# Layer 1's scans: u times D as matmuls, y copied out by ScalarE, four transfer slots, spread diagonals and piecewise loads

## The reference, cut to what matters

```
dA = exp(dt[:, :, None] * A)
h  = dA * h + (dt * u)[:, :, None] * B[:, None, :]
y  = einsum('bdn,bn->bd', h, C) + D * u
yh = y1 + y2 + y3 + y4        # y3, y4 turned back
```

## Time and profile before

| | us |
|---|---|
| median of 3 runs | 18361.85 (18345.74 to 18377.84) |
| the profiled execution's own time | 18362.69 |
| its span, first to last instruction | 18360.9 |
| busy over the span: PE, DVE, ACT, POOL | 16077.0, 15910.4, 14529.2, 11254.5 |
| mean granted TensorE clock | 0.962 |

### The profile page before, as it was taken

The page is one execution under the profiler, slowest core; times in us unless marked ns, Lnnn a source line. Parts: engine busy times, 40 slices in busy tenths (PEclk is TensorE's granted clock), DMA queues, the critical chain, the costliest instruction groups (busy, mean ns, idle before and its releaser), DMA issues. The chain is left out here.

```text
span 18360.9 us, 268147 instructions
## 1 busy us (share of the span) xinstructions
PE 16077.0 (88%) x94216; PEld 11444.0 (62%) x94216; DVE 15910.4 (87%) x12063; ACT 14529.2 (79%) x23238; POOL 11254.5 (61%) x6343
## 2 busy tenths in 40 slices
PE   8799998899996788879888888888888888889798
PEld 3355554455552365455688888888888888647374
DVE  4799998799996486479899999999999999879698
ACT  7699996799992555557899999999999999745556
POOL 0099993499990475035688888888888888500201
PEclk9899999899997899989999999999999999999899
DMA  5788886788879677767777777777777777741323
GB/s 178 231 243 250 246 252 208 233 249 247 251 223 245 213 226 217 265 230 278 224 191 200 194 192 191 194 193 192 191 190 197 197 191 191 194 122 55 104 57 101
DMA packets 1043305, 3693.66 MB, mean 201 GB/s; under 512 B 162006, under 2 KB 196410, under 8 KB 1017404
## 3 DMA queue, kind: packets, MB, share of 16 engines
q1 hardware_dynamic: 815420, 3003.46, 53.8%
q0 software_dynamic: 147456, 536.94, 14.9%
q10 hardware_dynamic: 79104, 136.10, 2.4%
HBM read 2342.15 MB, written 796.94 MB: 171 GB/s over the span
## 5 line engine op out<-in xcount | busy, mean ns | idle before, releaser
L1832 DVE TENSOR_TENSOR_SCAN l1s_h<-l1s_da,l1s_pd 128x1024 f32<-128x1024 f32 x3072 | 6709.3, 2262 | 152.0 <-DMA l1s_h<-l1s_h 85.4
L1853 ACT ACTIVATE l1s_da<-l1s_dl,l1s_a 128x1024 f32<-128x1024 f32 x3072 | 3505.0, 1141 | 312.7 <-DVE l1s_h L1832 308.5
L1718 PE MATMUL l1s_pd<-l1s_bd,l1s_dut 128*128 128x128 f32 x18432 | 2847.5, 291 | 853.7 <-DVE l1s_h L1832 828.6
L1718 PEld LDWEIGHTS l1s_pd<-l1s_bd,l1s_dut 128*128 128x128 f32 x18432 | 2297.3, 191 | 1229.0 <-DVE l1s_h L1832 1092.0
L1870 ACT ACTIVATE l1s_dm<-l1s_dut,l1s_bt 128x384 f32<-128x384 f32 x5120 | 2888.2, 602 | 200.9 <-PE l1s_pd L1723 200.5
L1687 POOL TENSOR_TENSOR l1s_pb<-l1s_h,l1s_cc 128x1024 f32<-128x1024 f32 x1024 | 2423.4, 2367 | 843.7 <-DVE l1s_h L1832 802.6
L1687 POOL TENSOR_TENSOR l1s_pa<-l1s_h,l1s_cc 128x1024 f32<-128x1024 f32 x1024 | 2428.0, 2371 | 84.1 <-DMA l1s_h<-l1s_h 84.1
L1723 PE MATMUL l1s_pd<-l1s_id,l1s_dm 128*128 128x128 f32 x15360 | 2186.6, 273 | 0.1
L2702 POOL TENSOR_TENSOR l0sf_pr<-l0sf_h,l0sf_cc 128x1024 f32<-128x1024 f32 x768 | 1810.9, 2375 | 32.2 <-DVE l0sf_h L2784 27.0
L2702 POOL TENSOR_TENSOR l0sb_pr<-l0sb_h,l0sb_cc 128x1024 f32<-128x1024 f32 x768 | 1809.1, 2371 | 30.8 <-DVE l0sb_h L2784 26.8
L1723 PEld LDWEIGHTS l1s_pd<-l1s_id,l1s_dm 128*128 128x128 f32 x15360 | 1789.4, 142 | 0.6 <-ACT l1s_dm L1870 0.5
(11 more groups left out here) (323 smaller groups left out, 31362.7 us busy)
## 6 DMA issues: line engine op xcount, KB each, us to landing
l1s_cc<-crows SPq DMA_DIRECT2D x1024, 512.0 KB, 4.5
l1s_h<-l1s_h POOLq DMA_DIRECT2D x1024, 512.0 KB, 6.9
l0sf_cc<-l0crowsf SPq DMA_DIRECT2D x512, 512.0 KB, 6.3
l0sb_cc<-l0crowsb SPq DMA_DIRECT2D x512, 512.0 KB, 5.7
l0sf_cc<-l0crowsf SPq DMA_DIRECT2D x512, 256.0 KB, 8.5
l0sb_cc<-l0crowsb SPq DMA_DIRECT2D x512, 256.0 KB, 7.6
dls<-l1p_dl SPq DMA_DIRECT2D x192, 512.0 KB, 7.0
duts<-l1p_dut SPq DMA_DIRECT2D x64, 1536.0 KB, 6.6
```

Source lines behind the costliest of these rows:

```text
L1718: pe.matmul(pd[:, s % 2, blk * 128:blk * 128 + 128], dut[:, half, blk, j * 128:j * 128 + 128], bd[:, n, blk - SCALED, :], start=True, stop ...
L1832: dve.tensor_tensor_scan(tile(rnd, j), da[:, j, :], pd[:, s % 2, :], 0.0, ALU.mult, ALU.add)\
L1853: act.activation(da[:, j, :], dl[:, half, j, :], ACT.Exp, scale=a[:, HT * half + j, n:n + 1])\
```

## The change

All edits but the last are in `l1_scans`.

- The term u x D moves to TensorE: matrices `dg` with the summed D on the diagonal are made once, and in rounds 24 to 27, step 0, `add_skip` adds the products of `u` with them to `py`, four blocks a round.
- `finish` moves from VectorE to ScalarE and becomes a plain copy of `py` to `yo`, at steps (2,1) and (3,2). TensorE's first accumulations of an image move to (2,2), (3,0), (4,0) and (4,1).
- The ring of the tile of step 1 grows from two to four, and `s_sum` from two to four semaphores.
- The diagonals of states 0 to 7 are made in rounds 17, 19, ... 31 of the image before, those of 8 to 15 in rounds 1, 3, ... 13 and 14. They wait for `bt` alone, which has semaphores of its own and is loaded in SyncE's round 5 (second half) and round 16 (first half of the next image). TensorE now waits itself for the loads of a half.
- The other loads are split: `dut` in four, `dl` in three, `u` in two pieces, one piece a round, from round 5 (nine pieces) and from round 18 (seven).
- ScalarE's products for the next round are split 1, 2, 2 over the steps in both halves.
- All 32 images are written out, with no loop.

```diff
-    STEP_BLOCKS = ((range(0, 1), range(1, 3), range(3, 5)), (range(0, 2), range(2, 4), range(4, 5)))
+    HALF_BLOCKS = (range(0, BLOCKS // 2), range(BLOCKS // 2, BLOCKS))
+    STEP_BLOCKS = (range(0, 1), range(1, 3), range(3, 5))
-    RINGS = (4, 2, 2)
-    TOGETHER = 3
-    LOADS = (3 * 16, 4 * 16)
+    RINGS = (4, 4, 2)
+    SUMS = 4
+    PIECES = (7, 9)
...
+        def diagonal_round(n):
+            return min(2 * n - (N - 1), N - 2)
...
         def images(eng, body):
-            body(0, True, False)
-            for i in range((IMAGES - 2) // TOGETHER):
-                for k in range(TOGETHER):
-                    body(i * TOGETHER + (k + 1), False, False)
-            body(IMAGES - 1, False, True)
+            for b in range(IMAGES):
+                body(b, b == 0, b == IMAGES - 1)
...
+                def load(b, half, piece):
+                    if piece < 4:
+                        at = piece * (BLOCKS // 4)
+                        cols = slice(at * HT * 128, (at + BLOCKS // 4) * HT * 128)
+                        sp.dma_start(dut[:, half, at:at + BLOCKS // 4, :],
+                                     duts[bass.ds(b, 1), half, :, cols].rearrange("a p n -> p (a n)")).then_inc(s_in[half], 16)
+                    elif piece < 7:
+                        sp.dma_start(dl[:, half, piece - 4, :], one(dls[:, HT * half + piece - 4], b)).then_inc(s_in[half], 16)
+                    else:
+                        sp.dma_start(u[:, piece - 7, :], one(u1[:, piece - 7], b)).then_inc(s_in[half], 16)
+
+                def load_bt(b, half):
+                    sp.dma_start(bt[:, half, :, :], bts[bass.ds(b, 1)].rearrange("a p n -> p (a n)")).then_inc(s_bt[half], 16)
...
                         if rnd == 5 and not first:
-                            load(b, 1)
-                        if rnd == 20 and not final:
-                            load(b + 1, 0)
+                            load_bt(b, 1)
+                        if 5 <= rnd < 5 + PIECES[1] and not first:
+                            load(b, 1, rnd - 5)
+                        if rnd == 16 and not final:
+                            load_bt(b + 1, 0)
+                        if 18 <= rnd < 18 + PIECES[0] and not final:
+                            load(b + 1, 0, rnd - 18)
...
+                def add_skip(b, part):
+                    j, blocks = part // 2, HALF_BLOCKS[part % 2]
+                    if part == 0:
+                        pe.wait_ge(skipd, nth(5))
+                        loaded(pe, b, 1)
+                    for blk in blocks:
+                        mm = pe.matmul(py[:, j, blk * 128:blk * 128 + 128], u[:, j, blk * 128:blk * 128 + 128], dg[:, j, :],
+                                       start=False, stop=False, skip_group_check=True)
...
-                        if j == 1 and not (first and rnd < 2):
-                            dve.wait_ge(s_sum[rnd % 2], summed(*((b, rnd - 2) if rnd > 1 else (b - 1, rnd + ROUNDS - 2))))
+                        if j == 1 and not (first and rnd < SUMS):
+                            dve.wait_ge(s_sum[rnd % SUMS], summed(*((b, rnd - SUMS) if rnd >= SUMS else (b - 1, rnd + ROUNDS - SUMS))))
...
-                        if rnd == 2 and j == 0 and not first:
-                            finish_b(b - 1)
-                        if rnd == 3 and j == 0 and not first:
-                            finish_a(b - 1)
...
+                def diagonals(b, n):
+                    if not (isinstance(b, int) and b == 0):
+                        act.wait_ge(trd, nth((b - 1) * STEPS + (N + n) * HT + HT - 1))
+                    act.wait_ge(s_bt[0], b * 16 + 16)
+                    for blk in range(SCALED, BLOCKS):
+                        ins = act.activation(bd[:, n, blk - SCALED, :], idt[:, :], ACT.Identity, scale=bt[:, 0, blk, n:n + 1])
+                    ins.then_inc(diagd, 1)
...
+                def finish(b, j, rows, back, fin):
+                    act.wait_ge(back, nth(b))
+                    act.activation(yo[rows, j * HW:j * HW + HW], py[rows, j, :], ACT.Identity).then_inc(fin, 1)
...
                             decay(b, rnd * HT + j)
                             if not first and (rnd, j) == (1, 1):
                                 hold(b - 1, 1, yb, heldb)
+                            if not first and (rnd, j) == (2, 1):
+                                finish_b(b - 1)
                             if not first and (rnd, j) == (2, 2):
                                 hold(b - 1, 0, ya, helda)
+                            if not first and (rnd, j) == (3, 2):
+                                finish_a(b - 1)
                             if ahead:
                                 times_b(m, v, blocks)
+                            if j == 0:
+                                for n in range(N):
+                                    if diagonal_round(n) % ROUNDS == rnd and not (final and diagonal_round(n) < 0):
+                                        diagonals(b if diagonal_round(n) >= 0 else b + 1, n)
```

More of the change, by code:

```diff
@@ L1601, in l1_scans @@
         s_in = [r.dma_sem(f"in{s}") for s in range(2)]
+        s_bt = [r.dma_sem(f"bt{s}") for s in range(2)]
         s_cc = [r.dma_sem(f"cc{s}") for s in range(4)]
@@ L1668, in _ @@
                 for half in range(2):
-                    load(0, half)
+                    load_bt(0, half)
+                    for piece in range(PIECES[half]):
+                        load(0, half, piece)
                 for rnd in range(3):
@@ L1715, in turn @@
                     pe.wait_ge(scan, nth(b * STEPS + s - 2))
-                    pe.wait_ge(diagd, nth(b * N + (N - 1 if half else n)))
+                    if n == 0 and j == 0:
+                        loaded(pe, b, half)
+                    pe.wait_ge(diagd, nth(b * N + n))
                     for blk in range(SCALED, BLOCKS):
@@ L1808, in _ @@
                 dve.wait_ge(skipd, nth(2))
-                def finish(b, j, rows, back, fin):
-                    dve.wait_ge(back, nth(b))
-                    dve.scalar_tensor_tensor(out=yo[rows, j * HW:j * HW + HW], in0=u[rows, j, :], scalar=dsum[rows, j, 0:1],
-                                             in1=py[rows, j, :], op0=ALU.mult, op1=ALU.add).then_inc(fin, 1)
-                def finish_b(b):
-                    finish(b, 1, slice(0, DHIGH), backb, finb)
-                def finish_a(b):
-                    finish(b, 0, slice(0, DLOW), backa, fina)
+                dve.memset(dg[DHIGH:, 1, :], 0.0).then_inc(skipd, 1)
+                for j, rows in ((0, slice(0, DLOW)), (1, slice(0, DHIGH))):
+                    dve.tensor_scalar(dg[rows, j, :], idt[rows, :], dsum[rows, j, 0:1], None, ALU.mult).then_inc(skipd, 1)
                 def body(b, first, final):
@@ L1860, in times_b @@
                             loaded(act, b, half)
-                        if half == 0:
-                            if not (isinstance(b, int) and b == 0):
-                                act.wait_ge(trd, nth((b - 1) * STEPS + (N + n) * HT + HT - 1))
-                            for blk in range(SCALED, BLOCKS):
-                                ins = act.activation(bd[:, n, blk - SCALED, :], idt[:, :], ACT.Identity,
-                                                     scale=bt[:, half, blk, n:n + 1])
-                            ins.then_inc(diagd, 1)
+                            act.wait_ge(s_bt[half], b * 16 + 16)
                         act.wait_ge(trd, nth(b * STEPS + (rnd - 1) * HT - 1))
@@ L1885, in body @@
                         m, v = b + (rnd + 1) // ROUNDS, (rnd + 1) % ROUNDS
-                        for j, blocks in enumerate(STEP_BLOCKS[v // N]):
+                        for j, blocks in enumerate(STEP_BLOCKS):
                             decay(b, rnd * HT + j)
@@ L3096 @@
     out = nc.dram_tensor("out", (IMAGES, C, HW), F32, kind="ExternalOutput").ap()
-    with nc.semaphore("sums0") as even, nc.semaphore("sums1") as odd:
-        build(nc, aps.pop("x"), aps, out, [even, odd])
+    with ExitStack() as stack:
+        build(nc, aps.pop("x"), aps, out, [stack.enter_context(nc.semaphore(f"sums{k}")) for k in range(4)])
     r = run_bass_kernel_spmd(nc, [{f"in_{name}": a for name, a in arrays.items()}], core_ids=[0])
```

47 lines of the change are left out of this document (24 added, 23 removed).

## The result

The changed kernel takes 18868.72 us (median of 4 runs, 18846.15 to 18884.48), the one before 18356.37 (4 runs). The ratio is 1.0279, 95% interval 1.0266 to 1.0291: slower, by 512 us. I had predicted 18,785, in the range 18,600 to 18,940.

What follows compares the result with a forecast made beforehand. VectorE's scans were taken to bound the stage; 18362.7 - 249.6 (gains) + 616.9 (A, B and C over 31 images) + 55.8 (clock) = 18785.8, given as 18,785 us, range 18,600 to 18,940.

Steps and rivals of the forecast that it cites:

- B: ScalarE's round 15 waits for the last piece of u; scan 46 late by 4.6 us an image, ends 2.5 to 6.7.
- C: ScalarE's round 17 diagonals wait for the next image's bt; scan 52 late by 11.1 us, ends 9.6 to 12.9.
- Rival 1: Pieces of the loads are in time, only gains show: 18,113 us, or 18,243 with A charged; chance 0.05.
- Rival 2: One of the two load waits is hidden: 18,615 us with C alone, 18,414 with B alone; chance 0.13.
- Rival 3: TensorE's clock stays low for a round after every hole and TensorE bounds there: +254, 19,040 us; chance 0.12.
- the decay as releaser: Sign on VectorE: its idle before scans should be released by the decay (l1s_da), some 600 us.
- Finishes off VectorE: Each image's two finishing instructions leave VectorE: 81.6 busy plus 54.2 waiting, 135.8 us saved.
- The 28.4 us of "issue": VectorE idle in 24 stretches before scans, put to the low clock after holes; all 28.4 us saved.
- Ring of four: Scans' wait on VectorE for the transfer folding two h tiles goes, with smaller pieces helping: all 85.4 us saved.
- A: ScalarE's copies out wait for TensorE's transposes back, making scans late: 4.2 us an image, ends 2.1 to 6.
- The clock: TensorE's granted clock drops after the holes of B and C: 0.9 us for each of 62, 55.8 in all.
- u x D on TensorE and the written-out images: Added TensorE products at step 0 of four rounds, and images as straight-line code: both taken as 0.

Runs made afterwards that it cites:

- x3: Changed kernel with both edits, next image's diagonals from round 21 and second half's loads from round 2, so no load is late: 18227.75 us.
- x1: Changed kernel with the diagonals of the next image's states 0 to 5 made from round 21 on, not 17, so bt is in time: 18528.53 us.
- x2: Changed kernel with the second half's bt and nine pieces issued from SyncE's round 2, not 5: 18579.61 us.
- x6: Kernel before with only the ring of four for step 1's tile and four semaphores for the transfer: 18385.46 us against 18357.27.
- x9: Kernel before with only the loads in pieces, from rounds 2 and 18, ring of two kept: 18246.80 us, ratio 0.9926.
- x10: x6 with the big loads whole but issued in different rounds (5, 7, 9 and 20, 22): 18231.89 us, ratio 0.9918 to the kernel before.
- x4: x3 with the first copy out moved on ScalarE behind round 2's third decay and the held copy, step (2,2): 18118.00 us.
- x7: x4 with the ring of step 1's tile and the transfer's semaphores back at two: 18148.18 us.
- x8: x3 with u x D and the finish back on VectorE, no products of u on TensorE: 18200.67 us.
- x5: Changed kernel with the last piece of u issued ahead of the spread of C in SyncE's round 13: 18758.96 us.

## Why the prediction was right, and where its terms were off

The mechanism was right: ScalarE comes to two loads before SyncE, which is behind it, has issued them (in the image shown 1.4 and 7.5 us before, 12053.39 and 12077.24), and both waits are shown by removing them one at a time. That the sum came within 84 us was in part luck: B and C both lay outside the ends that I had given for them, on opposite sides. Rival 1 (the pieces are in time) fell: x3 shows what it would have looked like, 18,228, near the 18,243 given for it. Rival 2 (one hidden) fell: each wait is there 31 times, and x1 and x2 add up in x3. Rival 3 fell too: the clock was back within the next round.

Of the signs, the decay as releaser (608.9 us), the 31 waits for bt (11.3 us each, 13 said) and the clock (0.95) came out; the 31 waits for u were 11.1 us each, where 6 to 8 had been said. Point by point, against the terms of the sum, with the totals of the stage from the section on the result:

- Finishes off VectorE, -135.8: they are gone from the list after, but were worth less in the stage. In the image of the earlier trace rows the first scan behind each starts 2.4 and 1.5 us later than the usual step of 2.18, which is 123 us for the 31 pairs that stand among the scans; the last pair stands behind them.
- The 28.4 us of "issue", said to be the clock's: 15.7 of them were five stretches of the kind that x6 shows, a scan behind GpSimd's wait for its spread. So the 1.2 us a hole that was read from them priced two things at once.
- Ring of four, "85.4 us, all of it": the amount is gone from the profile after, but the step gave it to the ring, and that was wrong. Alone the ring loses 28 us (x6), the loads apart make the gain (x9, x10), and the ring adds some 30 (x4 against x7). I had looked at who waits for the transfer and not at what else stood in SyncE's queue behind the same loads.
- A, 4.2 an image: 2.06 + 0.67 + 0.95 + 0.70 + 0.23 = 4.6 in the image shown, and 4.6 in all others: 13 us more. That the move gives nothing back was right (x8). Of it 3.5 us was the place of one copy (x4).
- B, 4.6 an image, 6.7 at most: measured 8.0 in the mean, and this is the term that was mis-sized most: 247.3 - 142.6 = 105 us. In the image shown it was 8.76: the piece landed 10.5 us after its issue, 10.9 after the spread's, not 6.6. I had taken 4.2 us a MB from a 1.5 MB load of before; this half MB took 4.7 us more than the spread, and the spread itself 6.2. x5 says that issuing it ahead of the spread takes 3.5 us off. How the rest divides between spread, piece and GpSimd's transfer (11.0 us here, 6.9 in the median before) was not measured by itself and stays open.
- C, 11.1 an image: measured 8.55 in the mean, since bt landed some 4 us after its issue and not 5.6. My lower end, that it lands with the spread, gave 9.6; in the image shown both landed together, but the spread took 3.6 us and not 4.5. That is 344.1 - 265.1 = 79 us less. The Trainium skill's fit ("DMA: Bandwidth & Descriptors", section "Anatomy of one DMA") gave 2.2 us for bt and so 7.6 for C, 1 us too low; the page gives it for a transfer that GpSimd issues, and bt is issued by SyncE. The trace has 3.5 us for bt here and 4.0 in the median of the stage.
- The clock, 0.9 a hole: 0.69 + 0.63 and 0.69 + 0.89 in the image shown, but 1.84 in the mean of all 62, twice what was said: 114.3 - 55.8 = 58 us more. The 0.66 had been taken from the first of the late scans, behind a hole of 2.39 us; here the second is late too, mostly by more than the first.
- u x D on TensorE and the written-out images, 0: in x4 the whole stage has 25 us of idling behind its first scan, so neither can cost more than that.

Together 105 - 79 + 13 + 58 = 97 us over the forecast. The stage grew by 531 where the sum had 423, 108 over; the finishes (13 us less gained) are about the rest. That the whole time is only 84 over (18,869 against 18,785) comes in part from the shorter work ahead of the stage, which no term of mine foresaw. B and C, off in opposite directions, hid most of each other.

## What to carry to other kernels

When each engine works down a list of its own, "round 16" is a different time on each. Before a load is moved, write down for its issuer and for its first reader when each reaches that round, from rows of the profile, and take the landing time between; here the issuer ran 4.9 us behind a round's end and the reader 3 to 4 us ahead of its start, and two waits of some 8 us an image on VectorE made a change that would have gained 132 us (x3) lose 512. A queue in order also delays what is issued behind a big load: look for the small periodic transfer behind it, not only for the one that is seen waiting. And an instruction that must wait belongs in a list where its turn comes when the wait is over; moving one copy by a step was worth 110 us (x4 against x3).

## What the runs showed of the hardware

- A spread of 512 KB behind 4 MB of loads in one queue landed 20.0 us after its issue in x6 (18.2 in an image of before), where the median of before is 4.5.
- A half MB load beside a spread and GpSimd's accumulating transfer of 512 KB each took 9.8 us in the median (7.2 to 14.3), where 1.5 MB issued together with more had taken 10.4. The pieces of dut, 384 KB each, took 8.2 us. Each piece was slow for its size, which costs nothing as long as no one waits for the last.
- After TensorE had stood idle for 8.69 us its granted clock was 0.50, and it was 1.00 again in 12074 to 12078, 7 to 11 us after the first scan behind the hole had started. Over the 62 holes of B and C the next two scans came late by 1.84 us together in the mean, 2.2 at most.
- A shorter wait does not always have that price. Behind the 2.06 us of A, TensorE's clock in x3 stayed at 1.00 in one image (12160 to 12174) and the later scans came 0.54 and 0.24 us late; in the next it was 0.69 in 12374 to 12378 and they came 0.96 and 0.67 us late.
